# Scan states written over the scan's input in PSUM, and the product by C directly behind the scan

## The reference, cut to what matters

```python
def step(h, inp):
    u_t, d_t, b_t, c_t = inp
    dA = jnp.exp(d_t[:, :, None] * A)
    h = dA * h + (d_t * u_t)[:, :, None] * b_t[:, None, :]
    y = jnp.einsum('bdn,bn->bd', h, c_t)
    return (h, y)
_, ys = jax.lax.scan(step, h0, xs)
return ys.transpose(1, 0, 2) + u * Dp
```

## Time and profile before

| | |
|---|---|
| median of three runs | 2012.53 us |
| the profiled execution's own time | 2010.69 us |
| its span | 2009.1 us |
| TensorE busy | 1811.3 us (90%) |
| VectorE busy | 1807.3 us (90%), of it scans 1146.3, products by C 327.5 |
| ScalarE busy | 1628.5 us (81%) |
| GpSimd busy | 1445.0 us (72%), of it products by C 692.7 |
| mean granted TensorE clock | 0.993 |

### The profile page before, as it was taken

One profiled execution on the slowest core, in us unless ns is written; L12 is line 12 of the kernel. 1 busy time (PEld: TensorE's weight loads), 2 busy tenths in 40 slices (PEclk: granted clock), 3 DMA queues, 4 the chain that ended last, 5 costly groups with the idle time before them and its releaser, 6 DMA issues. The chain is left out here.

```text
span 2009.1 us, 30384 instructions
## 1 busy us (share of the span) xinstructions
PE 1811.3 (90%) x10816; PEld 1139.7 (57%) x10816; DVE 1807.3 (90%) x1728; ACT 1628.5 (81%) x2957; POOL 1445.0 (72%) x1364
## 2 busy tenths in 40 slices
PE   6899999998988888998999999998986899999998
PEld 2444444444444444444444444444443699999997
DVE  3999999999999999999999999999999977777775
ACT  5999999999999999999999999999997434333332
POOL 2899999999999999999999999999999200000000
PEclk9999999999999999999999999999998999999999
DMA  8433333434343534433333333343435000000000
GB/s 266 95 77 95 77 95 78 109 84 101 88 106 80 115 81 94 95 77 95 77 95 77 95 78 96 85 107 78 107 65 155 1 12 12 12 11 12 6 4 9
DMA packets 79750, 155.88 MB, mean 78 GB/s; under 512 B 12016, under 2 KB 30064, under 8 KB 74992
## 3 DMA queue, kind: packets, MB, share of 16 engines
q1 hardware_dynamic: 73200, 135.52, 28.3%
q10 hardware_dynamic: 6400, 18.42, 3.0%
HBM read 128.86 MB, written 23.99 MB: 76 GB/s over the span
## 5 line engine op out<-in xcount | busy, mean ns | idle before, releaser
L801 DVE TENSOR_TENSOR_SCAN scan<-decay,dbu_ps 128x1024 f32<-128x1024 f32 x512 | 1146.3, 2268 | 64.5 <-issue 53.1
L463 POOL TENSOR_TENSOR scan<-scan,c_rep 128x1024 f32<-128x1024 f32 x255 | 692.7, 2716 | 104.1 <-DVE scan L801 104.1
L1026 PEld LDWEIGHTS dbu_ps<-ident,scan 128*128 128x128 f32 x4096 | 455.3, 141 | 437.6 <-DVE scan L801 208.0
L548 ACT ACTIVATE decay<-d_rep,a_cur 128x510 f32<-128x510 f32 x1024 | 664.7, 709 | 24.1 <-ACT dbc L572 12.0
L1026 PE MATMUL dbu_ps<-ident,scan 128*128 128x128 f32 x4096 | 552.0, 278 | 143.7 <-DVE scan L801 121.7
L457 POOL TENSOR_SCALAR scan<-du_t,b_t 128x256 f32<-128x256 f32 x896 | 561.6, 642 | 0.0
L616 ACT ACTIVATE scan<-du_t,b_t 128x256 f32<-128x256 f32 x1024 | 445.5, 494 | 2.6
L810 DVE TENSOR_TENSOR scan<-scan,c_rep 128x1024 f32<-128x1024 f32 x257 | 327.5, 1275 | 0.0
L740 ACT ACTIVATE decay<-dbu_ps 128x512 f32<-128x512 f32 x256 | 147.9, 597 | 203.2 <-PE dbu_ps L1225 182.8
L1011 PE MATMUL y_ps<-scan,sel 128*32 128x512 f32 x2048 | 274.7, 609 | 0.0
L1039 PE MATMUL pre_ps<-xn,w_pre 128*128 128x512 f32 x512 | 247.2, 606 | 5.0 <-DVE w_pre L790 5.0
(11 more groups left out here) (102 smaller groups left out, 1400.8 us busy)
## 6 DMA issues: line engine op xcount, KB each, us to landing
d_rep<-delta_rows SPq DMA_DIRECT2D x248, 256.0 KB, 5.9
c_rep<-c_rows SPq DMA_DIRECT2D x128, 256.0 KB, 4.5
delta_rows<-delta SPq DMA_DIRECT2D x62, 256.0 KB, 2.2
w_pre<-prepared_weights ACTq DMA_DIRECT2D x15, 866.0 KB, 4.4
prepared_weights<-scan SPq DMA_DIRECT2D x3, 1122.0 KB, 12.8
scan<-in_conv_w SPq DMA_DIRECT2D x4, 512.0 KB, 4.9
w_out<-prepared_weights SPq DMA_DIRECT2D x16, 128.0 KB, 2.1
sp_e<-in_x_rows SPq DMA_DIRECT2D x8, 256.0 KB, 3.5
```

Of the source, the lines that this page charges most:

```text
L463: nc.gpsimd.tensor_tensor(ring[slot % RING], ring[slot % RING], c_rep[par][:, slot // PRS, :].unsqueeze(1).broadcast_to([128, 2, TG]), ALU ...
L548: last = nc.scalar.activation(decay[slot % DEC][:, u, :, 1:], src[:, :, 1:], ACT.Exp, scale=a_cur[:, b, m:m + 1])
L801: nc.vector.tensor_tensor_scan(ring[slot % RING].rearrange("p u t -> p (u t)"), decay[slot % DEC].rearrange("p u a t -> p (u a t)"), dbu_p ...
L1026: last = nc.tensor.transpose(dbu_ps[slot % 2][:, u, 128 * j:128 * j + 128], dbu_t[m % 2][:, j, b, :, :].rearrange("p q c -> p (q c)"), ide ...
```

## The change

For even slots the scan now writes its states over its own input in `dbu_ps[0]`, and the product by C reads them from PSUM, together with C from SBUF, and writes the ring. Odd slots stay as they were. VectorE's order in a pair becomes scan, product, scan. The wait for free ring buffers (`quad_done`) moves from the even scan to its product. TensorE's transposes into `dbu_ps[0]`, and the experts' first matmuls into the same memory, wait for the product (`hc_dve`) where they waited for the scan; those into `dbu_ps[1]` still wait for the scan.

```diff
             def scan(s, slot):
-                if isinstance(s, int) and s == 0 and slot in (0, RING // 2):
+                if s == 0 and slot in (0, RING // 2):
                     dve.wait_ge(made_stored[2 + slot // (RING // 2)], 16)
                 dve.wait_ge(dbu_ready, SLOTS * s + slot + 1)
                 dve.wait_ge(decay_ready, SLOTS * s + slot + 1)
-                if slot % 2 == 0:
-                    wait(dve, quad_done, SLOTS // 2 * s + (slot - RING) // 2 + 1)
-                nc.vector.tensor_tensor_scan(ring[slot % RING].rearrange("p u t -> p (u t)"),
-                                             decay[slot % DEC].rearrange("p u a t -> p (u a t)"),
-                                             dbu_ps[slot % 2][:, :, :].rearrange("p u t -> p (u t)"), 0.0,
-                                             ALU.mult, ALU.add).then_inc(scan_done, 1)
+                inputs = dbu_ps[slot % 2][:, :, :].rearrange("p u t -> p (u t)")
+                states = inputs if slot % 2 == 0 else ring[slot % RING].rearrange("p u t -> p (u t)")
+                nc.vector.tensor_tensor_scan(states, decay[slot % DEC].rearrange("p u a t -> p (u a t)"),
+                                             inputs, 0.0, ALU.mult, ALU.add).then_inc(scan_done, 1)
 
             def times_c(s, i, par, slot):
                 if slot == 0:
                     dve.wait_ge(c_loaded[par], 16 * Q * (i + 1))
+                if slot % 2 == 0:
+                    wait(dve, quad_done, SLOTS // 2 * s + (slot - RING) // 2 + 1)
                 dve.wait_ge(scan_done, SLOTS * s + slot + 1)
-                nc.vector.tensor_tensor(ring[slot % RING], ring[slot % RING],
+                states = dbu_ps[0][:, :, :] if slot % 2 == 0 else ring[slot % RING]
+                nc.vector.tensor_tensor(ring[slot % RING], states,
                                         c_rep[par][:, slot // PRS, :].unsqueeze(1).broadcast_to([128, 2, TG]),
                                         ALU.mult).then_inc(hc_dve, 1)
 
                 for slot in range(SLOTS):
                     if has(s, 0):
                         scan(s, slot)
-                        if slot % 2:
-                            times_c(s, i, par, slot - 1)
+                        if slot % 2 == 0:
+                            times_c(s, i, par, slot)
...
-                wait(pe, scan_done, SLOTS * s + slot - 1)
+                if slot % 2:
+                    wait(pe, scan_done, SLOTS * s + slot - 1)
+                else:
+                    wait(pe, hc_dve, SLOTS // 2 * s + slot // 2)
...
-                        pe.wait_ge(scan_done, SLOTS * STEPS - 1 + c // 2)
+                        if c == 0:
+                            pe.wait_ge(hc_dve, SLOTS // 2 * STEPS)
+                        else:
+                            pe.wait_ge(scan_done, SLOTS * STEPS)
```

## The result

The changed kernel takes 2054.24 us (median of 4 runs, 2053.22 to 2057.29) against 2013.12 us: ratio 1.0205, 95% interval 1.0192 to 1.0219, slower by 41 us. The forecast was 2044 us, range 2018 to 2066. The profiled execution took 2054.28 us with a span of 2052.3 us.

The account below looks back on a forecast made before the run. One loop through VectorE, TensorE's queue and ScalarE was taken to set the step; 30 steps at 1.01 us more (30.3 us) plus 1.2 us at the end gave 2042.2 us profiled, 2044 us median; own range 2028 to 2054, overall 2018 to 2066.

Parts of the forecast that it names:

- The loop: Slot 8's scan, VectorE to slot 14, TensorE's queue, z and dbc projections, ScalarE's exponentials, next slot 8 scan: 1.01 us more per step.
- c4: TensorE's eight transposes for slot 4's scan, held by slot 2's product: start 32.46 us into the step, 1.01 us later.
- s8: VectorE's scan of slot 8, from which a step is counted; the next one forecast at 48.65 us instead of 47.64.
- c14: TensorE's eight transposes for slot 14's scan, now waiting for slot 12's product: start at 14.82 us instead of 13.42.
- c2: TensorE's transposes for slot 2's scan, at the end of a 12.93 us queue: start at 27.75 us, 0.91 us later.
- t2's end: End of VectorE's product by C for slot 2, which releases slot 4's transposes: forecast at 32.40 us.
- The bubble: VectorE's pause between an even scan and its dependent product: start 0.04 us past the scan's end, 0.11 us per pair.
- The stall in front of s2: New VectorE gap before slot 2's scan, waiting for its transposes: 0.75 us a step.
- The wait and the order: TensorE's even-slot transposes wait for products rather than scans, with VectorE's new order; counted together, slot 2's transposes 0.91 us later.
- the case of a whole pass: PSUM writes cost each even scan 1.12 us, making VectorE the bound: 7.2 us a step, about 2260 us.
- GpSimd's relief: GpSimd's products no longer meet VectorE's, falling to 2.37 us; as a rival, 0.49 us a step saved, 1998 us, chance 0.14.
- The faster rival: GpSimd's earlier outer products end TensorE's idle time before slot 0's transposes: 0.49 us a step saved, 1998 us, chance 0.14.

Follow-up runs that it names:

- a late c14: Kernel before, old order, states in SBUF; only TensorE's transposes of slot 14 wait for the scan of slot 13 instead of slot 12: 2095.82 us.
- two pairs put back: Changed kernel with slots 2 and 12 returned to states in the SBUF ring, old order scan, scan, product and the old wait: 2039.22 us.
- the first experiment: Kernel before with only VectorE's order changed to scan, product, scan; states stay in the SBUF ring, transposes still wait for the scan: 2123.09 us.
- the run with the product late: Changed kernel with VectorE's old order scan, scan, product; even states in PSUM, transposes wait for the product: 2556.46 us.
- slot 8: Kernel before with TensorE's convolution halves one slot earlier, dbc projection before slot 4's transposes, and the change in slot 8 alone: 1996.86 us.

## Why the prediction was right, point by point

*The loop.* Right. From c4 to the next s8 it is 16.2 us in the kernel before, in the changed one (550.37 to 566.54), with a late c14 and with two pairs put back, so all that moves in these lies in front of c4. A late c14 by itself, in the old order, moves the step (49.1 us), and two restored pairs of eight give back half.

*The terms*, counted from s8, in the changed kernel: c14 15.09 us (14.82 forecast), c2 27.80 (27.75), s2 28.93 (28.90), t2's end 32.55 (32.40), c4 32.70 (32.46), the next s8 48.87 (48.65). The loss per step is 1.23 us, forecast 1.01. That c2 fits so well is luck: c14 came 0.27 us later than forecast, and the queue from c14 to c2 took 12.71 us (27.80 - 15.09) instead of 12.93. The miss arises behind s2: its pair ends 0.12 us later against s2 than forecast, and c4 starts 0.15 us behind t2's end, not 0.06.

*The bubble* was mis-sized. I took 0.04 us past the scan's end from a pair in SBUF; behind a scan that writes PSUM it is 0.10 to 0.11 us. With states in SBUF, in the new order, it is 0.03 (480.44 + 2.29 against 482.76 in the first experiment), so some 0.07 us belong to the states' place in PSUM. The product behind its scan is 1.22 us, not 1.19, but that isn't PSUM's price: in the same place it is 1.22 us from SBUF too (482.76), and behind the odd scan 1.20 us from PSUM (the run with the product late). The pair is 5.71 us (523.40 to 529.11), not 5.63. The Trainium skill's page "Perfetto Trace Analysis", section "Optimizing Scalar/DVE Operations", which has PSUM some 65 ns dearer per instruction than SBUF, came nearer for the scan and the start behind it than my zero; for the product's reading no run here shows a price. As a whole PSUM paid: against states in SBUF, in the same order, it saves 1.6 us a step.

*The stall in front of s2* was mis-sized: 0.26 us, forecast 0.75, since VectorE with its dearer pairs got there later itself. It is no term of the loop's sum.

*The wait and the order were one item in my sum and are two causes.* With c14 waiting for the scan it could start at 13.77 us, but c15 needs s13, which now stands behind t12 and ends at 17.23; TensorE reaches c15 at 17.74 as it is. Worked out from that, some 0.46 us of c2's 0.96 are the wait's, the rest is the odd scan's new place. No run separates the two: without the wait the states may not lie in PSUM, and in SBUF the meetings with GpSimd hide it.

*The sum.* In 28 of the 31 intervals between two s8, and in one more near the end (46.40 to 47.64), the loss is 1.24 us; the first loses 1.8, the last, which I had not counted, 0.8 (48.20 to 49.04). The first s8 comes 1.4 us later (76.68 against 75.25), two of the 28 lose another 0.67 each to the clock, and the end takes 1.8 us (I had 1.2). Together 43 us of span against 31.5 forecast. Two figures around the forecast don't come out of their own terms: its range, with 13 us off, begins at 2031 and not 2028, and the case of a whole pass, where VectorE's 7.2 us a step would have stood in place of the loop's 1.01 and not on top of it, gives about 2230 and not 2260.

*GpSimd's relief* came as said, 2.37 us for every product, and brought nothing in the changed kernel, where GpSimd is not in the loop. That it is worth something where a meeting stands in VectorE's path is shown by slot 8. The faster rival's condition was a queue from c14 to c2 more than 0.9 us shorter than 12.93; it was 0.22 us shorter, and c14 came 1.67 us later than before. The idle time in front of c0 did go, but it was the late c14 that filled it.

## What to carry to other kernels

When an engine's result is left in a buffer that another engine refills, look at when the last reader is done, not the writer, and follow the refiller's queue to the next engine that already waits on it: there the step pays what the queue's own idle time doesn't absorb (here 1.47 of 2.18 us), however idle the engines look. Moving one operand to PSUM takes a VectorE instruction out of the way of GpSimd; here it paid in the one slot whose timeline showed a meeting on the path (1997 us) and not in all eight (2028 us with TensorE's list in the same order). A gain that an experiment fails to show may have turned into a new meeting, which the length of single instructions shows and the waits don't.

## What the runs showed of the hardware that was not expected

TensorE's granted clock drops inside a busy loop. In the kernel before no step but the first and the last has a drop. In the changed kernel two more steps have one. The windows below are of the first of them (columns: TensorE, its weight loads, VectorE, ScalarE and GpSimd busy us, granted clock, DMA share, GB/s). The clock is at 1.00 (2.4 GHz) and then at 0.50, the level of 1.2 GHz, for 3.4 us, in which eight transposes take 1.94 us instead of 1.09. One step earlier the stretch that corresponds to the first window (359.33 to 368.63) has the same 7.78 us of TensorE's work in 9.30, and no drop follows; what decides between the two is not shown.

```profile
408.20:417.50 9.30, 7.78 (x49) 4.00 (x47) 9.20 (x6) 9.22 (x16) 7.16 (x10) 1.00 0.58 143
417.90:421.30 3.40, 3.40 (x16) 1.63 (x16) 2.05 (x1) 3.40 (x7) 3.40 (x4) 0.50 0.75 187
```

```profile
417.79 1.94 PE L1030 MATMUL dbu_ps<-ident,scan 128*128 128x128 f32 x8 [1.04 <-DVE scan L801]
```

A step whose clock fell takes 0.7 us more in the changed kernel (49.55) and 1.7 us more with a late c14, where the drop comes behind a wait of 3.40 us and hits the queue that sets the step. There the wait added to TensorE costs twice: 1.5 us a step by itself, and 1.7 more where the clock falls behind it.

VectorE and GpSimd stand behind each other for a whole instruction when each reads two tensors from SBUF: 3.15 and 2.61 us for a product of VectorE's that takes 1.2. Who started first goes ahead: VectorE at 513.81 with GpSimd at 513.97, GpSimd at 487.54 with VectorE at 488.39 and at 221.28 with VectorE at 221.58. In the last of these a shift of 1.8 us, the gap in front of s8, had made the meeting. In the changed kernel, with one input of VectorE's product in PSUM, none of GpSimd's 255 products is longer than 2390 ns.
